# First attention of a fused kernel: the query, key and value weights loaded in 128-byte pieces and transposed by VectorE

## What is computed

```python
Bx  = einsum('bni,bri->bnr', x, B[ids])          # rank 16
c   = einsum('bnr,bor->bno', Bx, A[ids])         # 512 features
qkv = einsum('sbh,ph->sbp', c, weight_qkv)       # 8 groups x (4 q + 1 k + 1 v) x 128
attn over s = 8 positions, causal; out = einsum('sbe,he->sbh', attn_out, weight_proj)
x = x + out
```

## Time and profile before

| | |
|---|---|
| time, median of 3 runs | 1568.53 us (1563.63 to 1569.09) |
| the profiled execution's own time | 1554.2 us |
| its span | 1552.5 us |
| TensorE busy | 1509.9 us (97%), 8984 matmuls |
| VectorE, ScalarE, GpSimd busy | 1180.2, 893.2, 879.2 us |
| DMA packets, bytes | 74085, 133.39 MB |
| first attention | from the start to about 300 us; its later iterations take 34.05 us each |

### The profile page before, as it was taken

The page is one execution under the profiler, slowest core; times in us unless marked ns, Lnnn a source line. Parts: engine busy times, 40 slices in busy tenths (PEclk is TensorE's granted clock), DMA queues, the critical chain, the costliest instruction groups (busy, mean ns, idle before and its releaser), DMA issues.

```text
span 1552.5 us, 27376 instructions
## 1 busy us (share of the span) xinstructions
PE 1509.9 (97%) x8984; PEld 1293.2 (83%) x8984; DVE 1180.2 (76%) x2668; ACT 893.2 (58%) x2308; POOL 879.2 (57%) x1231
## 2 busy tenths in 40 slices
PE   6899999989999999999999999999999999999997
PEld 4788888778888888888888888888888888888885
DVE  3666665767888888888888878888887888777865
ACT  2433333356666666666666666666666666666641
POOL 1111234236667666766676676667666766676521
PEclk8999999999999999999999999999999999999999
DMA  6654555322222222222222222222222222311102
GB/s 209 209 161 134 148 165 162 77 82 70 69 71 73 69 71 61 76 70 70 64 72 71 71 66 70 70 71 72 70 72 66 70 69 65 89 59 48 42 27 82
DMA packets 74085, 133.39 MB, mean 86 GB/s; under 512 B 17426, under 2 KB 27026, under 8 KB 73946
## 3 DMA queue, kind: packets, MB, share of 16 engines
q1 hardware_dynamic: 56482, 97.56, 21.2%
q0 software_dynamic: 16464, 33.85, 7.5%
q10 hardware_dynamic: 1000, 0.23, 0.1%
HBM read 107.47 MB, written 7.34 MB: 74 GB/s over the span
## 4 chain that ended last, share of the span: by engine, by line
PE 91%; DVE 3%; ACT 2%; issue 2%; POOL 1%; DMA 1%; ACTq 0%; POOLq 0%; DVEq 0%; SPq 0%
PE ps_t L948 15%; PE ps_o L739 11%; PE ps_o L741 10%; PE ps_o L740 10%; PE ps_b L739 5%; PE ps_b L741 5%; PE ps_b L740 5%; PE ps_q L741 4%; PE ps_q L740 4%; PE ps_q L739 4%; PE ps_t L762 3%; PE ps_a L739 3%; PE ps_a L793 3%; PE ps_a L741 3%; PE ps_a L740 3%
## 5 line engine op out<-in xcount | busy, mean ns | idle before, releaser
L1443 ACT ACTIVATE sm<-sm,mn 128x640 f32<-128x640 f32 x256 | 211.4, 826 | 234.5 <-DVE mn L1912 234.5
L1788 DVE TENSOR_TENSOR pT_lo<-ps_t,pT_hi 128x512 fp32r<-128x512 f32 x320 | 220.2, 688 | 113.5 <-ACT pT_hi L1366 113.3
L622 POOL DMA_INDIRECT kraw<-in_L_cond_k_cache_dram,idx_a x200 | 197.5, 988 | 89.1 <-issue 74.3
L1366 ACT ACTIVATE pT_hi<-ps_t 128x512 fp32r<-128x512 f32 x320 | 188.5, 589 | 84.7 <-PE ps_t L948 84.7
L622 POOL DMA_INDIRECT vraw<-in_L_cond_v_cache_dram,idx_a x200 | 198.7, 994 | 59.6 <-issue 59.3
L948 PE MATMUL ps_t<-ident,sm 128*128 128x128 f32 x1280 | 195.7, 275 | 3.2 <-ACT sm L1453 1.5
L948 PEld LDWEIGHTS ps_t<-ident,sm 128*128 128x128 f32 x1280 | 147.9, 140 | 51.4 <-DVE qT_lo L1788 17.9
L639 POOL TENSOR_TENSOR z<-pairs_p,zl 128x128 f32<-128x128 f32 x160 | 57.9, 402 | 206.8 <-DVE pairs_p L1652 206.8
L739 PE MATMUL ps_o<-pT_lo,v_hi 128*128 128x512 f32 x320 | 129.8, 406 | 0.0
L741 PE MATMUL ps_o<-pT_hi,v_hi 128*128 128x512 f32 x320 | 125.5, 392 | 0.0
L740 PE MATMUL ps_o<-pT_hi,v_lo 128*128 128x512 f32 x320 | 124.9, 390 | 0.0
(11 more groups left out here) (257 smaller groups left out, 4370.1 us busy)
## 6 DMA issues: line engine op xcount, KB each, us to landing
fv<-st SPq DMA_DIRECT2D x128, 128.0 KB, 2.3
tab<-tab_scratch SPq DMA_DIRECT2D x64, 256.0 KB
wraw<-n_L_attn_weight_qkv_dram SPq DMA_DIRECT2D x8, 1536.0 KB, 7.3
wpraw<-_L_attn_weight_proj_dram SPq DMA_DIRECT2D x8, 1024.0 KB, 9.4
mask<-mask_scratch SPq DMA_DIRECT2D x64, 128.0 KB
wtile<-in_L_cond_Wq_dram SPq DMA_DIRECT2D x28, 256.0 KB
wtile<-in_L_cond_Wo_dram SPq DMA_DIRECT2D x28, 256.0 KB
kraw<-in_L_cond_k_cache_dram,idx_a POOLq DMA_INDIRECT x200, 2.6
```

The source lines that it names most:

```text
L622: pool.indirect_dma_start(raw[:, par, c, :], None, rows_d, bass.IndirectOffsetOnAxis(idx[:, k:k + 1].bitcast(U32), 0)).then_inc(arrived[pa ...
L1366: act.activation(dst, src, ACT.Copy).then_inc(t_hi, 1)
L1443: act.activation(sm[:, h, :], sm[:, h, :], ACT.Exp, bias=mn[:, h:h + 1], scale=-1.0, accum_out=den[:, h:h + 1]).then_inc(e_done, 1)
L1788: dve.tensor_tensor(lo, src, hi.bitcast(F32), ALU.subtract).then_inc(t_lo, 1)
```

## The change

One `wraw` instead of two, two `wT` instead of one. A load is four transfers of 3072 pieces of 32 floats: 32 neighbouring columns of one row go to one partition, so that VectorE can turn 32x32 blocks, 24 at a time, with 4 instructions a group (one for 128 columns of all 768 rows). TensorE's W groups, ScalarE's `w_copy` and their places in the ring are gone. `aall` is loaded with columns in natural order, in pieces of 64 bytes instead of 256. VectorE turns a group one ahead; SyncE waits for `w_turned` before it overwrites `wraw`.

```diff
-        wraw = [at("wraw0", [P, 6, HID], F32, 148), at("wraw1", [P, 6, HID], F32, 0)]
+        wraw = at("wraw", [P, 6, HID], F32, 148)
-        wT = at("wT", [P, 6, NC_, P], F32, 136)
+        wT = [at("wT0", [P, NC_, 6 * P], F32, 136), at("wT1", [P, NC_, 6 * P], F32, 0)]
...
-        T_FIRST = ["W0", "W1", "W2", "W3", "W4", "W5", "P0", "P1", "P2", "P3"]
-        T_BOTH = ["W0", "W1", "W2", "W3", "W4", "W5", "Z0", "Z1", "P0", "P1", "Z2", "P2", "P3", "Z3", "Z4"]
+        T_FIRST = ["P0", "P1", "P2", "P3"]
+        T_BOTH = ["Z0", "Z1", "P0", "P1", "Z2", "P2", "P3", "Z3", "Z4"]
...
             def load_w(g):
-                sp.dma_start(wraw[g % 2][:], w_qkv[g * 6 * P:(g + 1) * 6 * P, :].rearrange("(t p) o -> p t o", p=P)
-                             ).then_inc(wq_in[g % 2], 16)
+                blocks = w_qkv[g * 6 * P:(g + 1) * 6 * P, :].rearrange("(b k) (c i a) -> i b k c a", b=32, c=NC_, i=4)
+                for i in range(4):
+                    sp.dma_start(wraw[32 * i:32 * i + 32, :, :].rearrange("b t (j c a) -> b (t j) c a", j=4, c=NC_),
+                                 blocks[i]).then_inc(wq_in, 16)
...
-                sp.dma_start(aall[:, n, :, :].rearrange("p j r -> p (j r)"),
-                             lora_a[bass.ds(a_id, 1), :, :].rearrange("a (p j) r -> (a p) (j r)", j=NC_)
+                sp.dma_start(aall[:, n, :, :],
+                             lora_a[bass.ds(a_id, 1), :, :].rearrange("a (j p) r -> (a p) j r", j=NC_)
                              ).then_inc(lora_in, 16)
+            load_wp(1)
+            sp.wait_ge(w_turned, 4)
             load_w(1)
-            load_wp(1)
...
+                if g >= 1 and g + 2 < G:
+                    sp.wait_ge(w_turned, 4 * (g + 2))
+                    load_w(g + 2)
                 for h in range(HG):
                     scatter(g, h)
                 if g + 2 < G:
-                    load_w(g + 2)
+                    if g == 0:
+                        sp.wait_ge(w_turned, 8)
+                        load_w(2)
                     load_wp(g + 2)
...
             def fold(g, t):
-                pe.wait_ge(w_done, 6 * g + t + 1)
+                if t == 0:
+                    pe.wait_ge(w_turned, 4 * (g + 1))
...
             for i in range(1, G):
-                w_group(i, 0)
-                w_group(i, 1)
-                fold(i, 0)
-                w_group(i, 2)
-                fold(i, 1)
...
+                for t in range(4):
+                    fold(i, t)
                 z_group(i, 0)
                 fold(i, 4)
...
+            def turn(g, cs=range(NC_)):
+
+                for c in cs:
+                    if c == 0:
+                        dve.wait_ge(wq_in, 64 * (g + 1))
+                        if g >= 2:
+                            dve.wait_ge(fold_full, g - 1)
+                    dve.transpose(wT[g % 2][:, c, :].rearrange("p (b k) -> p k b", b=32),
+                                  wraw[:, :, :].rearrange("p t (j c a) -> p (t j) c a", j=4, c=NC_)[:, :, c, :]
+                                  ).then_inc(w_turned, 1)
...
             dve.memset(score[:], NEG).then_inc(smx0, 1)
+            turn(0)
...
             soft_sum(0)
+            turn(1)
             for i in range(1, G):
+                if 1 < i < G - 1:
+                    turn(i + 1)
                 z_low(i, 0)
...
                 x2_sum(i, 2)
+                if i == 1:
+                    turn(2, [0])
...
                 x2_sum(i, 3)
+                if i == 1:
+                    turn(2, [1])
...
                 x2_sum(i, 4)
+                if i == 1:
+                    turn(2, [2])
...
                 x2_sum(i, 5)
+                if i == 1:
+                    turn(2, [3])
```

More of the change, by code:

```diff
@@ L229, in block_program @@
         idx_ok = sem("idx_ok")
-        wq_in = [sem(f"wq_in{i}") for i in range(2)]
+        wq_in = sem("wq_in")
         wp_in = [sem(f"wp_in{i}") for i in range(2)]
-        w_full = sem("w_full")
-        w_done = sem("w_done")
+        w_turned = sem("w_turned")
         p_full = sem("p_full")
@@ L384, in t_freed @@
             kind, j = name[0], int(name[1])
-            if kind == "W":
-                return w_done, 6 * i + j + 1
             if kind == "P":
@@ L506, in _ @@
                 if g + 2 < G:
-                    load_w(g + 2)
+                    if g == 0:
+                        sp.wait_ge(w_turned, 8)
+                        load_w(2)
                     load_wp(g + 2)
                 if g == G - 2:
-                    sp.dma_start(wraw[0][:, 0:HG, :], wq[0:QW, :].rearrange("(t p) i -> p t i", p=P)
+                    sp.wait_ge(w_turned, 4 * G)
+                    sp.dma_start(wraw[:, 0:HG, :], wq[0:QW, :].rearrange("(t p) i -> p t i", p=P)
                                  ).then_inc(w0_in, 16)
-                    sp.dma_start(wraw[0][:, HG, :], wk[0:P, :]).then_inc(w0_in, 16)
-                    sp.dma_start(wraw[0][:, HG + 1, :], wv[0:P, :]).then_inc(w0_in, 16)
+                    sp.dma_start(wraw[:, HG, :], wk[0:P, :]).then_inc(w0_in, 16)
+                    sp.dma_start(wraw[:, HG + 1, :], wv[0:P, :]).then_inc(w0_in, 16)
                     sp.dma_start(wpraw[0][:], wo[:, 0:QW].rearrange("(t p) e -> p t e", p=P)).then_inc(w0_in, 16)
@@ L763, in ring @@
                 return mm
[L765 to L769, removed]
             def p_group(g, h):
@@ L783, in c_group @@
                     pe.wait_ge(w0_in, 64)
-                ring(G, f"C{t}", [wraw[0][:, t, c * P:(c + 1) * P] for c in range(NC_)]).then_inc(w0_full, 1)
+                ring(G, f"C{t}", [wraw[:, t, c * P:(c + 1) * P] for c in range(NC_)]).then_inc(w0_full, 1)
             def fold(g, t):
-                pe.wait_ge(w_done, 6 * g + t + 1)
+                if t == 0:
+                    pe.wait_ge(w_turned, 4 * (g + 1))
                 if g >= 1 and t == 0:
@@ L792, in fold @@
                 for j in range(NC_):
-                    mm = pe.matmul(ps_a[:, t * P:(t + 1) * P], wT[:, t, j, :], aall[:, :, j, :],
+                    mm = pe.matmul(ps_a[:, t * P:(t + 1) * P], wT[g % 2][:, j, t * P:(t + 1) * P], aall[:, :, j, :],
                                    start=(j == 0), stop=(j == NC_ - 1))
@@ L861, in _ @@
                 mm.then_inc(zT_full, 1)
-            w_group(0, 0)
-            w_group(0, 1)
             pe.wait_ge(zT_done, 2)
@@ L870, in _ @@
             pe.wait_ge(lora_in, 16 * N)
[L871 to L880, removed]
+            for t in range(6):
+                fold(0, t)
             p_group(0, 0)
@@ L900, in _ @@
             for i in range(1, G):
-                w_group(i, 0)
-                w_group(i, 1)
-                fold(i, 0)
-                w_group(i, 2)
-                fold(i, 1)
[L906 to L909, removed]
-                w_group(i, 5)
+                for t in range(4):
+                    fold(i, t)
                 z_group(i, 0)
@@ L1262, in ring @@
                 return ps_t[t_pos(i, name) % 2]
-            def w_copy(g, t):
-                act.wait_ge(w_full, 6 * g + t + 1)
-                act.activation(wT[:, t, :, :], ring(g, f"W{t}")[:, :].rearrange("p (c b) -> p c b", c=NC_), ACT.Copy
-                               ).then_inc(w_done, 1)
             def p_copy(g, h):
@@ L1315, in _ @@
             act.activation(cos_t[:], cos_t[:], ACT.Sin).then_inc(sin_ok, 1)
-            for t in range(6):
-                w_copy(0, t)
             fold_copy(0)
@@ L1329, in _ @@
             for i in range(1, G):
-                for t in range(6):
-                    w_copy(i, t)
                 z_copy(i, 0)
```

## The result

The changed kernel takes 1587.09 us (median of 4 runs, 1581.31 to 1590.06) where the kernel before, run beside it, takes 1568.81. The ratio is 1.0123 (95%: 1.008 to 1.0166): slower, by more than the interval, though by less than 2%. One of the four runs of the kernel before took 2129.24 us, and the ratio leaves it out. A second set of runs (the last experiment) gave 1.0114 (1.0097 to 1.013). The forecast was 1565.8, no change; the time lies inside its range of 1556 to 1591. The profiled execution has a span of 1578.0 us, against 1552.5.

A forecast was written before the change was run, and what follows sets the result against it. TensorE was taken to bound the kernel, 97% busy. Terms 0 + 2.7 + 1.7 + 9.4 - 16.5 gave -2.7 us against the profiled 1554.2; carried over to the runs' median, 1565.8, no change; range 1556 to 1591.

The forecast's parts named there:

- the transpose: VectorE's turn of 768 columns: 0.96 us each, 3.84 a group, hidden in steady iterations with 0.8 us over.
- Dearer transposes: Rival: at 1.9 us a transpose the kernel gets slower, about +20 us in total; chance 0.08.
- the cover: VectorE's idle 7.33 us at an iteration's start, to hide the turns; short by 3.0 in four iterations at 1.9 us each.
- the start: Group 0, before its folds: transposes of 1.9 us each would cost 3.5 us more than the forecast's 0.
- the single turns: Four single transposes in VectorE's dense part of iteration 1: cost 1.7 us, at 1.9 us each 4 more.
- Dearer pieces: Rival: small load pieces cost more, slower; total +6 at 14.4 us a load, +15 at 17.3, +29 at 22; chance 0.27.
- What an iteration gains: Iterations 2 to 7: without TensorE's W groups 7.34 us become 4.05, each iteration giving 3.3 us.
- The stand in iteration 2: TensorE stands 10.2 us before `z_out(2)`, as scatters into `fv` queue behind the moved wait and `load_w(3)`.
- Small pieces: Loads of `wraw` in 128-byte pieces: 11.2 us a load, where it was 3.9.
- Scatters pass quickly: Rival: in iteration 2 scatters start 2.4 us after the wait, TensorE stands 2.9; total -12.5 us; chance 0.20.
- Start cost 0: Group 0: `wraw` lands at 25.7, `turn(0)` ends at 29.5, before `zlT`'s second half at 30.52; cost 0, 0.3 us over.
- The clock after a pause: TensorE at half clock for some 5 us after iteration 2's stand, 2.5 more; iteration 1's loss taken as equal to before.

The follow-up runs named there:

- the last experiment: The changed kernel once more, unaltered, with more rounds beside the kernel before: 1573.32 us, ratio 1.0114.
- the dense runs: The changed kernel with each transpose reading and writing 768 neighbouring columns, of four bytes (1560.68 us) or of two bytes (1559.29 us, ratio 0.9968).
- the four kernels with the order as changed: Changed kernel's load and scatter order, with transposes: neighbouring columns 1560.68 us; two-byte 1559.29; output alone dense 1547.74; whole computation dense 1563.78.
- the two kernels with the order changed: Four scatters issued ahead of `load_w(3)` and its wait, `turn(2)` in two halves: on the dense whole computation 1553.04 us, on the changed kernel 1566.15 us.
- the first profile: Profiled execution of the changed kernel as first measured against the kernel before: span 1578.0 us; timed median 1587.09 us, ratio 1.0123.
- the second profile: Profile of the changed kernel run again unaltered against the kernel before: 1573.32 us, ratio 1.0114.
- the first set: Kernel before repeated, and changed kernel with half the transposes, neighbouring columns or two-byte elements, run on one chip; the kernel before took 1563.67 us.

## Why the prediction was wrong

The step that failed is the price of **the transpose**: "256 columns cost 0.26 and 768 take 0.96. I take that". It measured 2.11 us, and in a row one every 1.9. The 0.96 was worked out from instructions that write neighbouring columns, and for a transpose that does so it is right to 3% (0.938, 0.937, 0.936 us in three kernels). The change's transpose writes to every 24th column, and I had no term for that. The bound from above, 1.9, was near, but for a wrong reason (two passes for 4-byte data, refuted by the dense runs with both widths). The Trainium skill's page Vector Engine (DVE) Microarchitecture Reference (The reshape front-end and per-opcode configuration), by whose one element a cycle per lane I held the dearer transpose to be ruled out, says this of the reorder array that stands ahead of the engine's lanes. The dense runs fit it (768 columns in 0.938 us, where 512 columns from two inputs take 0.69). That sentence does not speak of how the output is written, so it could not rule out 2.11 us, and I read too much into it.

The rival *Dearer transposes* had the mechanism and nearly the size: "about +20" at 1.9 us, against 18 to 19 (ratios 1.0114 and 1.0123) and 15 to 20 in the traces. It was given 0.08. Its four parts: the cover short by 3.0 us, measured 2.87, in each of iterations 3 to 6; `turn(1)` 3.8 more, measured 3.9 (first fold at 66.12, forecast 62.2); the start 3.5, measured 0.1 and 1.5 (by the end of `soft_sum(0)` in the two profiles), because the load came 3.0 and 1.6 us earlier than I had it; the single turns 4 more, measured 1.8 more (from the first `z_out` of iteration 1 to the end of that iteration 27.6 us, before 24.1, forecast 1.7 longer). So its mechanism held, and it priced the start and the single turns too high. That the time lies inside the stated range is in part luck: 0.27 of the chance on the slower side stood on *Dearer pieces*, which did not come, and 0.08 on what did.

The other steps:

- **What an iteration gains.** Right. 3.3 us, where nothing covers it up: iteration 7, and the steady iterations with half the transposes (all at 30.72) or dense ones (30.72 to 31.2 in the four kernels with the order as changed).
- **The stand in iteration 2.** Forecast 10.2, measured 10.3, in part by luck: SyncE was held for 7.5 us and not 9.7, and the 16 scatters took 12.0 and not 10.1. Nor is `fv` the only cause. I had `turn(3)` through before it; with slow transposes `turn(3)` and `z_low` end just 1 us before `fv`. With dense ones it is as I had it: `fv` comes last, 4.63 us behind. That the order makes it is shown by the two kernels with the order changed.
- **Small pieces.** Somewhat too dear. The forecast of 11.2 us a load was to land some 13 after its issue; from the issue of `load_w(3)` to the first turn it is 11.41. At the start the turns began at 22.73 and 24.14, where I had the landing at 25.7. (The line through both sizes gives 0.0142 us a piece and 10.9 us, not 0.0145 and 11.2.) The rival *Dearer pieces* is out. The estimate of 12.7 us by the rule of the Trainium skill's page DMA: Bandwidth & Descriptors (How a descriptor splits into AXI transactions) was too dear as well; whether the rule or my price of a piece is off, no run here shows.
- **Scatters pass quickly.** They do not: 12.04 us for 16, behind 7.49 for the load's four issues.
- **Start cost 0.** Right in the first profile: the first fold of group 0 is 0.6 us later, 0.4 of it because TensorE's own product ends later (30.86, before 30.48), and `soft_sum(0)` ends 0.1 later. In the second profile the turns end at 31.95, behind the time when `zlT` could be made; the first fold is 1.9 later and `soft_sum(0)` ends 1.5 later.
- **The clock after a pause.** I counted it in iterations 1 and 2 only. Behind iteration 2's stand it cost about 1.4 (the +1.0 of the third row, less 2.87 of standing, plus 3.3), where I had 2.5. It also follows the steady iterations' pauses in some cases, where I had no pause and so no term.

## What to carry to other kernels

Before an operation is priced from rows of others, compare the access patterns too, output first: what is cheap into neighbouring columns can take more than twice the time into a strided view (0.94 and 2.11 us here). Here the stride could be moved into the load's order, where it cost some 3 us once and saved 2.9 an iteration. An operation put into another engine's idle time is free only while it fits; and the cover has to be measured as the change leaves it. VectorE's idle time was 7.3 us, but only 4.7 were left once TensorE had less to do; 7.8 us of turns gave back 2.9 of the 3.3 us gained, and 3.6 us of turns kept it all. When one queue issues both a load that waits for a consumer and transfers that the next stage needs, their order can decide whether the change pays (6 us here with slow turns; with fast ones 10, between no change and 0.65% faster).

## What was not expected of the hardware

- A VectorE transpose of 128x768 in 32x32 blocks takes 0.94 us into neighbouring columns and 2.11 us into every 24th column, with the input's jumps or without; dense, four-byte and two-byte elements take the same.
- Four transfers of 3072 pieces of 128 bytes hold SyncE for 15.52 us at the start and 7.5 to 11.0 later, with 2 KB pieces for 2.87 and 1.7; yet in iteration 2 the turns that wait for the data start only 2 us later. Sixteen transfers of 768 such pieces hold it for 10.6 to 18.6 us.
- A pause of TensorE of 2.87 us is followed by the full clock in some iterations (33.78 us in all) and by about 6 us at half clock in others (36.66).
- The part behind the first attention, which no kernel here changes, takes 1223 to 1226 us in some profiles and 1231 to 1236 in others, along with the time of the kernel before in the same set (1553.9 and 1555.6, or 1563.7 and above). Within the first set it takes 1231.7 us in the kernel before and 1234.1 to 1235.7 in three kernels with turns; no other set can tell whether that is the change's doing. The profile of before shown above is of the former kind (its own time is 1554.2), that of the changed kernel of the latter. In the changed kernel's first profile TensorE waits 29 times for ScalarE's `kvown`, in its second 8 times. Whether the chip is the reason for a set's kind stays open.
